# Second attention: the high and low parts of queries and keys are made by GpSimd from a whole copy that ScalarE writes

## The chip, the cores and the metric

The kernel runs on one core of a Trainium2 chip. The metric is the device time of one execution in microseconds (us), the median of the runs shown. One execution was profiled; every row below is from it. Engines: PE is TensorE's matmul, PEld its weight load, DVE is VectorE, ACT is ScalarE, POOL is GpSimd, SP is SyncE, which issues all DMAs spoken of here.

## The reference, cut to what matters

Sixteen sequences of 512 rows by 256 columns go through four layers, each with a residual: a first attention, a feed-forward layer with FP4 rounding, a second attention, and the feed-forward layer again. The change is in the second attention alone:

```python
Q = einsum('bsh,nhd->bnsd', x, Wq) + bq        # 8 heads of 32
K = einsum('bsh,nhd->bnsd', x, Wk) + bk
V = einsum('bsh,nhd->bnsd', x, Wv) + bv
qq, kq = Q @ Wc2q + bc2q, K @ Wc2q + bc2q      # 8 numbers for each row and head
fid = (qq . kq) / max(|qq| |kq|, 1e-8)
qw = fid * (1 + 0.1 * sin(pi * fid))
cw = (Q . K) / sqrt(32)
probs = softmax(0.5 * qw + 0.5 * cw)
attn = (probs @ V) @ Wo + bo
x1 = layernorm(x + attn, g1, beta1)
qm = (x1 @ W1 + b1) @ Wm + bm
qe = tanh(qm) * cos(qm * pi / 4)
out = layernorm(x1 + (qe @ Wqo + bqo) @ W2 + b2, g2, beta2)
```

## The kernel before

The four layers run one after the other. In the second attention (`attention_b`) each engine has its own program, a loop of bodies `s` = -1 to 16, one for each sequence and some at the ends. The order of all work is written out by hand: a body has 16 slots `n`, each with four places `j`. Places of slots 0 to 7 hold the eight groups (two halves of heads `c`, four row tiles) of sequence s: `score_head` on PE, `total_max` on DVE, `exps` on ACT; the turning of the probabilities (`turn_head`, `move_turned`) and their product with V (`weigh`) lag one and two slots behind. Slots 8 to 15 hold the cosine term of the next sequence s+1: `dots` on PE, `sines` on ACT, `cosine_term` on DVE, two heads at a time, which hand the score banks from one engine to the next. Between these stand the side jobs of the list `B_JOBS`, one matmul group each into one of three PSUM banks (S, T0, T1), moved out by DVE or ACT as the two `MOVES` tables say. Those that matter here, with their place in PE's body:

```python
    (0, 3, "B0", "S", 1),     # code projections of sequence s+1
    (1, 3, "N0", "S", 1),     # their squared norms
    (5, 0, "G0", "S", 1),     # turns the inverse norms rn8, spread by GpSimd
    (5, 2, "R0", "S", 0),     # turns the inverse sums of the first half of heads
    (8, 1, "Q0", "S", 1), (9, 3, "K0", "T0", 1),     # queries, keys of s+1, half 0
    (10, 3, "y0", "S", 0), (11, 1, "y1", "T0", 0),   # output projection of s
    (13, 3, "Q1", "S", 1), (14, 1, "K1", "T0", 1),   # queries, keys of s+1, half 1
```

Scores are made from numbers split into a high part, rounded to the matmul's fp32r type, and a low part, the rest. For each of Q0, K0, Q1 and K1, ACT (line 2070) writes the high part `part[:, i, 0, :]`, the PSUM bank plus the bias, and DVE (line 1963) writes the low part `part[:, i, 1, :]`, the bank plus the bias less the high part, and frees the bank. When K of a half is freed, SP's `place(s, c)` (lines 1749 to 1756) copies the parts with six DMAs into `stack`, the operand of `score_head`; half 0 is wanted at slot 0 of the next body, half 1 at slot 4.

GpSimd's body is a fixed queue: `inverse_norms` (line 1831, a power; waits until N0 is moved), `spread_norms` (line 1818, writes `rn8`, which G0 reads), `spread_sums(s, 0)` (line 1827, for R0), `add_row2`, `low_part` (line 1835, the low part of the code units), `spread_sums(s, 1)`, `rstd_of(s + 2, 0)` (line 1799), `add_row1` (line 1842, waits until y1 is moved), `rstd_of(s, 1)` (line 1792), `applied(x1)` (lines 1807 to 1813), `rstd_of(s - 1, 2)`, `applied(x2)`, `residual` (line 1852).

Of the kernel before, what the change touches and what calls it, by code (L numbers as in the profile page):

```python
# [7 lines left out]
ALU = mybir.AluOpType  # L8
# [3 lines left out]
P = 128  # L12
# [1603 lines left out]
def attention_b(nc, s_passed, ident, consts, w, u, kept, front, x_from, x_to, head):  # L1616
    ctx = ExitStack()
    with ctx:
# [27 lines left out]
        hi, lo, units = head.hi, head.lo, head.units  # L1646
        part = sb("part", [P, 2, 2, SEQ], FP32R)
        stack = sb("stack", [P, 2, 2, 4, SEQ], FP32R)
        v = sb("v", [P, TILES, H])
        negmax = sb("negmax", [P, B_GROUPS, 4])  # L1650
        sums = sb("sums", [P, 2, TILES, 4])
# [29 lines left out]
        s_xr = sem("residual_input_ready")  # L1681
        s_sq, s_rn, s_rn8 = head.s_sq, head.s_rn, head.s_rn8
        s_uhi, s_ulo, s_qs = head.s_uhi, head.s_ulo, head.s_qs
        s_hi = sem("high_part_ready")
        s_placed = sem("parts_placed")
        s_dots = sem("dots_ready")
        s_sin = sem("sines_ready")
# [33 lines left out]
        @block.sync  # L1721
        def _(sp):
            def one(ap, q):
                return ap.rearrange("s (t p) h -> p (s t) h", p=P)[:, bass.ds(q * TILES, TILES), :]

            def load_next(q):
                wait(sp, s_xh, 4 * q)
                sp.dma_start(xin[:], one(x_from, q)).then_inc(s_xin, 16)

            def load_again(q):  # L1730
                wait(sp, s_store, 16 * q)
                sp.dma_start(xres[:], one(x_from, q)).then_inc(s_xres, 16)

            def store_x(q):
                sp.wait_ge(s_add, q + 1)
                sp.dma_start(one(x_to, q), xres[:]).then_inc(s_store, 16)

            def place_units(q):

                sp.wait_ge(s_uhi, q + 1)  # L1740
                sp.sem_inc(s_passed, 1)
                wait(sp, s_dots, 32 * q)
                for src, blocks_ in ((hi, ((0, 0), (0, 1), (1, 0), (1, 2))), (lo, ((0, 2), (0, 3), (1, 1), (1, 3)))):
                    if src is lo:
                        sp.wait_ge(s_ulo, q + 1)
                    for i, b in blocks_:
                        sp.dma_start(units[NQ * b:NQ * (b + 1), i, :, :], src[64 * i:64 * i + 64, :]).then_inc(s_qs, 16)

            def place(s, c):

                freed(sp, s, f"K{c}")
                sp.sem_inc(s_passed, 1)
                wait(sp, s_score, 32 * s + 16 + 16 * c)
                for i, order in enumerate(((0, 0, 1), (0, 1, 0))):
                    for b, h in enumerate(order):
                        sp.dma_start(stack[32 * b:32 * b + 32, i, c, :, :].bitcast(FP32),
                                     part[:, i, h, :].bitcast(FP32)).then_inc(s_placed, 16)

            def body(s):
                if has(s + 2):  # L1760
                    load_next(s + 2)
                if has(s) and has(s + 1):
                    place_units(s + 1)
                if has(s - 2):
                    store_x(s - 2)
                if has(s - 1):
                    load_again(s - 1)
                if has(s + 1):
                    place(s, 0)
                    place(s, 1)  # L1770
                if s == SEQS - 1:
                    sp.wait_ge(s_turn, 32 * s + 16)
                    sp.sem_inc(s_passed, 1)
                    for dst, src in kept:
                        sp.dma_start(dst, src).then_inc(s_kept, 16)
                    sp.wait_ge(s_turn, 32 * s + 28)
                    sp.sem_inc(s_passed, 1)
                    sp.dma_start(front.x_of(0), one(x_to, 0)).then_inc(front.s_x, 16)

            b_bodies(sp, body, 2)  # L1780
            store_x(SEQS - 1)
            sp.wait_ge(s_kept, 16 * len(kept))
            sp.wait_ge(s_store, 16 * SEQS)

        @block.gpsimd
        def _(pool):
# [28 lines left out]
            def spread_norms(q):  # L1815
# [3 lines left out]
                                 rn[:].rearrange("p (b h) -> p b h", h=B_HEADS).unsqueeze(2)  # L1819
                                 .to_broadcast([P, 2 * TILES, NQ, B_HEADS])).then_inc(s_rn8, 1)  # L1820

            def spread_sums(s, c):

                wait(pool, s_o, 2 * s + c)
                pool.wait_ge(s_inv, 2 * s + c + 1)
                src = inv_sums[:].rearrange("p t h -> p (t h)").unsqueeze(2).to_broadcast([P, 4 * TILES, HD])
                pool.tensor_copy(rec[:].rearrange("p t (h d) -> p (t h) d", d=HD), src).then_inc(s_rec, 1)
# [26 lines left out]
            def body(s):  # L1854
                if has(s) and has(s + 1):
                    inverse_norms(s)
                    spread_norms(s + 1)
                if has(s):
                    spread_sums(s, 0)
                if has(s - 1):  # L1860
                    add_row2(s - 1)
                if has(s) and has(s + 1):
                    low_part(s + 1)
                if has(s):
                    spread_sums(s, 1)
                if has(s + 2):
                    rstd_of(s + 2, 0)
                if has(s + 1):
                    add_row1(s)
                if has(s):  # L1870
                    rstd_of(s, 1)
                if s == SEQS - 1:
                    front.pool_norm(pool, 0)
                if s == SEQS:
                    front.pool_scale(pool, 0)
                if has(s):
                    applied(x1, s, 1, G1, BETA1, s_x1)
                if has(s - 1):
                    rstd_of(s - 1, 2)
                    applied(x2, s - 1, 2, G2, BETA2, s_x2)  # L1880
                    residual(s - 1)
                if s == SEQS - 1:
                    front.pool_divide(pool, 0)
# [4 lines left out]
        def _(dve):  # L1888
# [53 lines left out]
            def move_side(s, job):  # L1942
# [6 lines left out]
                if job == "z1":  # L1949
                    dve.tensor_copy(zT[:, 1, :], side).then_inc(done, 1)  # L1950
                elif job == "B0":
                    wait(dve, s_ulo, q)
                    dve.tensor_scalar(out=base[:], in0=side, scalar1=w["bqk"][:], scalar2=None,
                                      op0=ALU.add).then_inc(done, 1)
                elif job == "N0":
                    dve.tensor_scalar(out=n2[:], in0=side[:, 0:64], scalar1=NORM2_MIN, scalar2=None,
                                      op0=ALU.max).then_inc(done, 1)
                elif job == "G0":
                    dve.tensor_tensor(out=base[:], in0=base[:], in1=side, op=ALU.mult).then_inc(done, 1)
                elif job[0] in "QK":  # L1960
                    i = "QK".index(job[0])
                    dve.wait_ge(s_hi, 4 * q + 2 * c + i + 1)
                    dve.scalar_tensor_tensor(out=part[:, i, 1, :], in0=side, scalar=w[("bq", "bk")[i]][:, c:c + 1],
                                             in1=part[:, i, 0, :], op0=ALU.add, op1=ALU.subtract).then_inc(done, 1)
                elif job[0] == "y":
                    dve.wait_ge(s_xr, q + 1)
                    wait(dve, s_row2, q)
                    dve.tensor_tensor(out=x1[:, d, :], in0=pair, in1=xr[:, d, :], op=ALU.add).then_inc(done, 1)
                elif job == "m0":
                    dve.tensor_tensor(out=qm[:], in0=side[:, 0:TILES * NQ].rearrange("p (t q) -> p t q", q=NQ),  # L1970
                                      in1=w["bm"][:].unsqueeze(1).to_broadcast([P, TILES, NQ]),
                                      op=ALU.add).then_inc(done, 1)
                elif job == "t0":
                    dve.tensor_copy(qeT, side[0:NQ, :]).then_inc(done, 1)
                else:
                    dve.wait_ge(s_row2, q + 1)
                    dve.tensor_tensor(out=x2[:, d, :], in0=pair, in1=x2[:, d, :], op=ALU.add).then_inc(done, 1)
# [26 lines left out]
            def reciprocals(s, c):  # L2004
# [1 line left out]
                wait(dve, s_rec, 2 * s + c)  # L2006
                dve.reciprocal(out=inv_sums[:], in_=sums[:, c, :, :]).then_inc(s_inv, 1)

            MOVES = {(1, 0): "B0", (2, 0): "N0", (3, 3): "z1", (5, 1): "G0", (6, 3): "m0", (8, 3): "Q0", (10, 1): "K0", (10, 3): "t0",
                     (11, 1): "y0", (11, 3): "y1", (12, 1): "f0", (12, 3): "f1", (14, 1): "Q1", (14, 3): "K1"}  # L2010

            def body(s):
                for n in range(B_SLOTS):
# [34 lines left out]
        def _(act):  # L2048
            def move_side(s, job):
# [16 lines left out]
                    act.activation(zT[:, 0, :], side, ACT.Copy).then_inc(done, 1)  # L2066
                elif job[0] in "QK":
                    i = "QK".index(job[0])
                    wait(act, s_placed, 96 * (2 * q + c))
                    act.activation(part[:, i, 0, :], side, ACT.Identity,  # L2070
                                   bias=w[("bq", "bk")[i]][:, c:c + 1]).then_inc(s_hi, 1)
                elif job[0] == "V":
                    act.activation(v[:, 2 * c:2 * c + 2, :], side.rearrange("p (a h) -> p a h", a=2),
                                   ACT.Copy).then_inc(done, 1)
# [348 lines left out]
```

## Time and profile before

| | us |
|---|---|
| median of 3 runs | 3481.36 |
| lowest and highest run | 3473.24, 3483.72 |
| the profiled execution | 3484.37 |
| its span | 3482.6 |
| PE busy | 3049.3 (88%) |
| DVE busy | 2696.7 (77%) |
| ACT busy | 2123.2 (61%) |
| POOL busy | 1576.3 (45%) |

The shares are averages over four layers with different limits. Queries and keys of the second attention are moved between 1670 and 2847 us of the span, so a change there is read from that stage, one body after the other, and from what each engine waits for in it.

### The profile page before, as it was taken

What the parts mean: (1) busy time and instruction counts of PE and PEld (TensorE: products, weight loads), DVE (VectorE), ACT (ScalarE), POOL (GpSimd) and SP (SyncE); (2) the same over time, 40 slices, a digit from 0 to 9 for tenths busy, and PEclk for the clock granted to TensorE, in tenths of its full rate; (3) what the DMA queues carried; (4) which work ended last, traced back from release to release, by engine and by line L of the source; (5) the groups of instructions that cost most, each with busy time, mean ns of one, the idle gap of its engine ahead of it and who ended that gap; (6) DMA issues with size and microseconds to landing.
All of it is one profiled execution on the core that took longest, in us unless ns stands there. A gap on an engine that the chain in (4) does not pass through costs nothing. (4 is left out here: it accounts for less than half of the span.)

```text
span 3482.6 us, 70085 instructions
## 1 busy us (share of the span) xinstructions
PE 3049.3 (88%) x23640; PEld 2358.0 (68%) x23640; DVE 2696.7 (77%) x6902; ACT 2123.2 (61%) x5264; POOL 1576.3 (45%) x1287
## 2 busy tenths in 40 slices
PE   5998999999985999997789989888988993899998
PEld 3666666666664888887456656666665662788888
DVE  4666666666666999995688888888888883899997
ACT  3777777777772344343677777777778782344443
POOL 4323223232203555554135666655556655455554
PEclk9999999999996999998899999999999996999999
DMA  5354353543423000000434444444454441111100
GB/s 91 53 77 66 56 77 57 74 68 53 72 36 120 13 19 13 19 19 17 63 55 74 67 75 73 61 74 67 67 74 69 72 84 51 37 37 37 32 24 25
DMA packets 133654, 193.45 MB, mean 56 GB/s; under 512 B 15110, under 2 KB 81030, under 8 KB 132614
## 3 DMA queue, kind: packets, MB, share of 16 engines
q1 hardware_dynamic: 133302, 188.96, 31.8%
q8 instruction: 196, 3.21, 0.4%
q14 instruction: 156, 1.28, 0.2%
HBM read 45.12 MB, written 28.84 MB: 21 GB/s over the span
## 5 line engine op out<-in xcount | busy, mean ns | idle before, releaser
L476 ACT ACTIVATE a_probs<-a_probs,a_negmax 128x176 f32<-128x176 f32 (+4 forms) x1024 | 502.7, 491 | 250.5 <-DVE a_negmax L402 246.5
L402 DVE CUSTOM_DVE_ANT_0 a_probs<-a_mask,a_score 128x176 f32<-128x176 f32 (+4 forms) x1024 | 404.3, 400 | 308.2 <-PE a_turned L560 149.8
L560 PE MATMUL a_turned<-ident,a_probs 128*128 128x128 f32 (+1 forms) x2176 | 403.3, 279 | 52.2 <-DVE a_pT L411 25.6
L1996 DVE CUSTOM_DVE_ANT_0 b_u<-b_u,b_score 128x512 f32<-128x512 f32 x512 | 341.0, 682 | 130.1 <-PE b_score L2235 126.7
L2109 ACT ACTIVATE b_u<-b_u,b_negmax 128x512 f32<-128x512 f32 x512 | 367.1, 718 | 106.8 <-DVE b_negmax L1996 105.6
L1493 PE MATMUL f_y_bank<-f_wdT,f_hqT 128*128 128x256 f32 x1536 | 362.8, 387 | 41.7 <-ACT f_hqT L1424 38.3
L1288 POOL TENSOR_TENSOR f_hq<-f_h_mark,f_nscale 128x704 f32<-128x704 f32 x128 | 177.6, 1387 | 407.4 <-DVE f_h_mark L1357 407.4
L1988 DVE SCALAR_TENSOR_TENSOR b_u<-b_u,b_score 128x1024 f32<-128x1024 f32 x256 | 310.4, 1217 | 65.9 <-ACT b_u L2102 60.9
L2102 ACT ACTIVATE b_u<-b_score 128x1024 f32<-128x1024 f32 x256 | 261.9, 1024 | 158.6 <-PE b_score L2225 157.0
L1493 PEld LDWEIGHTS f_y_bank<-f_wdT,f_hqT 128*128 128x128 f32 x1536 | 288.7, 192 | 91.4 <-issue 56.8
L336 POOL COPY a_rec<-a_inv_sums 128x512 f32<-128x512 f32 x32 | 19.5, 610 | 703.4 <-DVE a_inv_sums L416 703.4
L2244 PE MATMUL b_turned<-ident,b_u 128*128 128x128 f32 x2048 | 318.0, 280 | 14.2 <-DVE b_pT L2002 10.5
L560 PEld LDWEIGHTS a_turned<-ident,a_probs 128*128 128x128 f32 (+1 forms) x2176 | 236.6, 134 | 127.7 <-ACT a_probs L476 62.7
L1417 ACT ACTIVATE f_h_mag<-f_hu 128x704 f32<-128x704 f32 x128 | 100.8, 788 | 333.0 <-POOL f_hu L1280 333.0
L2244 PEld LDWEIGHTS b_turned<-ident,b_u 128*128 128x128 f32 x2048 | 245.7, 143 | 85.4 <-issue 47.9
L1476 PE MATMUL f_gate<-f_wguT,f_xqT 128*128 128x352 f32 x1536 | 286.0, 336 | 0.0
L1476 PE MATMUL f_up<-f_wguT,f_xqT 128*128 128x352 f32 x1536 | 280.7, 332 | 0.0
L2235 PE MATMUL b_score<-b_stack 96*128 96x512 f32 x512 | 256.9, 513 | 25.5 <-DVE b_u L1988 25.5
L1476 PEld LDWEIGHTS f_gate<-f_wguT,f_xqT 128*128 128x128 f32 x1536 | 251.8, 194 | 0.2
L1476 PEld LDWEIGHTS f_up<-f_wguT,f_xqT 128*128 128x128 f32 x1536 | 248.0, 191 | 0.0
L411 DVE COPY a_pT<-a_turned 128x256 f32<-128x256 f32 (+3 forms) x512 | 223.8, 437 | 3.6 <-PE a_turned L560 1.4
L551 PE MATMUL a_score<-a_stack_k,a_stack_q 112*128 112x512 f32 (+3 forms) x512 | 207.3, 416 | 1.5 <-DVE a_negmax L402 1.5
(271 smaller groups left out, 7274.0 us busy)
## 6 DMA issues: line engine op xcount, KB each, us to landing
b_stack<-b_part SPq DMA_DIRECT2D x192, 256.0 KB, 7.8
a_stack_q<-a_part SPq DMA_DIRECT2D x192, 128.0 KB, 4.4
a_wide_k<-a_part SPq DMA_DIRECT2D x96, 164.0 KB, 7.8
a_stack_k<-a_part SPq DMA_DIRECT2D x96, 128.0 KB, 4.7
xs<-in_x_dram SPq DMA_DIRECT2D x16, 512.0 KB, 10.4
x_before_b<-xs SPq DMA_DIRECT2D x16, 512.0 KB, 2.9
b_units<-b_hi_lo SPq DMA_DIRECT2D x128, 64.0 KB
b_xres<-x_before_b SPq DMA_DIRECT2D x16, 512.0 KB, 3.8
```

What stands on the lines that cost most here:

```text
L402: dve.tensor_tensor_reduce(out=probs[:, n % 2, j, 0:keys(n)], in0=mask_of(n), in1=score[j][:, 0:keys(n)], scale=-1.0, scalar=3.0e38, op0=A ...
L411: dve.tensor_copy(pT[:, n % 2, j, 0:t, :], turned[0][:, 0:t, :]).then_inc(s_mv_v, 1)
L476: act.activation(probs[:, n % 2, j, 0:keys(n)], probs[:, n % 2, j, 0:keys(n)], ACT.Exp, bias=negmax[:, n, j:j + 1], scale=-1.0, accum_out= ...
L560: m = nc.tensor.transpose(turned[j % 2][0:rows, u, :], chunk(n, probs[:, n % 2, j, :], u), ident[:])
L1476: m = mm(dst[:, a, 0:HALF], xqT[:, i, k, t * P:(t + 1) * P], wguT[:, j, k, at:at + HALF], start=p == 0, stop=p == len(products) - 1)
L1493: m = mm(y_bank[:, 0:H], hqT[:, t % 2, c * P:(c + 1) * P], wdT[:, c, :], start=c == 0, stop=c == IC - 1)
L1988: dve.scalar_tensor_tensor(out=u[:, g, d, :], in0=u[:, g, d, :], scalar=10.0, in1=score[:, d, :], op0=ALU.add, op1=ALU.mult).then_inc(s_u, 1)
L1996: dve.tensor_tensor_reduce(out=u[:, n, j, :], in0=u[:, n, j, :], in1=score[:, j, :], scale=-0.05, scalar=3.0e38, op0=ALU.add, op1=ALU.min, ...
L2102: act.activation(u[:, g, d, :], score[:, d, :], ACT.Sin, scale=PI_IN).then_inc(s_sin, 1)
L2109: act.activation(u[:, n, j, :], u[:, n, j, :], ACT.Exp, bias=negmax[:, n, j:j + 1], scale=-1.0, accum_out=sums[:, c, t, j:j + 1]).then_inc ...
L2235: mm(score[:, j, :], stack[0:96, 0, c, j, t * P:(t + 1) * P], stack[0:96, 1, c, j, :], start=True, stop=True).then_inc(s_score, 1)
L2244: m = nc.tensor.transpose(turned[j % 2][:, t, :], u[:, n, j, t * P:(t + 1) * P], ident[:])
```

## The change

ACT writes the whole value, bank plus bias, to a new fp32 buffer `whole_part[:, i, :]`, waits for its own write, frees the bank, and raises `s_whole`. GpSimd gets two calls of a new function `split`, one for each half `c`: for queries and then keys it copies the whole value to the high part, waits for that, and subtracts the high part from the whole value into the low part. The calls stand behind `spread_sums(s, 1)` and behind `applied(x1)`. The four moves of DVE are gone, also from its `MOVES` table. SP's `place` waits for the second low part of a half in place of the freed bank.

```diff
+        whole_part = sb("whole_part", [P, 2, SEQ])
...
             def place(s, c):
 
-                freed(sp, s, f"K{c}")
+                sp.wait_ge(s_low, 2 * (2 * (s + 1) + c + 1))
...
+            def split(q, c):
+
+                wait(pool, s_placed, 96 * (2 * q + c))
+                for i in range(2):
+                    step = 2 * (2 * q + c) + i + 1
+                    pool.wait_ge(s_whole, step)
+                    pool.tensor_copy(part[:, i, 0, :], whole_part[:, i, :]).then_inc(s_hi, 1)
+                    pool.wait_ge(s_hi, step)
+                    tt(out=part[:, i, 1, :], in0=whole_part[:, i, :], in1=part[:, i, 0, :],
+                       op=ALU.subtract).then_inc(s_low, 1)
...
                     spread_sums(s, 1)
+                if has(s + 1):
+                    split(s + 1, 0)
                 if has(s + 2):
                     rstd_of(s + 2, 0)
...
                     applied(x1, s, 1, G1, BETA1, s_x1)
+                if has(s + 1):
+                    split(s + 1, 1)
                 if has(s - 1):
                     rstd_of(s - 1, 2)
...
-                elif job[0] in "QK":
-                    i = "QK".index(job[0])
-                    dve.wait_ge(s_hi, 4 * q + 2 * c + i + 1)
-                    dve.scalar_tensor_tensor(out=part[:, i, 1, :], in0=side, scalar=w[("bq", "bk")[i]][:, c:c + 1],
-                                             in1=part[:, i, 0, :], op0=ALU.add, op1=ALU.subtract).then_inc(done, 1)
...
                     i = "QK".index(job[0])
-                    wait(act, s_placed, 96 * (2 * q + c))
-                    act.activation(part[:, i, 0, :], side, ACT.Identity,
-                                   bias=w[("bq", "bk")[i]][:, c:c + 1]).then_inc(s_hi, 1)
+                    wait(act, s_low, 2 * (2 * q + c - 1) + i + 1 if 2 * q + c else 0)
+                    act.activation(whole_part[:, i, :], side, ACT.Identity,
+                                   bias=w[("bq", "bk")[i]][:, c:c + 1]).then_inc(done, 1)
+                    freed(act, s, job)
+                    act.sem_inc(s_whole, 1)
```

## Rows read from the trace of the kernel before

**Rows 1.** Groups by line, 1900 to 2800 us: count, busy, mean; idle before, releaser.

```profile
L1963 DVE SCALAR_TENSOR_TENSOR b_part<-b_turned,b_bk,b_part 128x512 fp32r<-128x512 f32 x24 | 17.9, 746 | 0.0
...
L1827 POOL COPY b_rec<-b_inv_sums 128x512 f32<-128x512 f32 x23 | 14.1, 612 | 184.1 <-DVE b_inv_sums L2007 183.9
...
L1835 POOL TENSOR_TENSOR b_hi_lo<-b_base,b_hi_lo 128x512 f16<-128x512 f32 x11 | 12.8, 1164 | 16.3 <-ACT b_hi_lo L2060 16.3
```

**Rows 2.** POOL's groups by line and shape, whole span; columns as in rows 1.

```profile
L296 POOL TENSOR_TENSOR a_square<-a_square 128x512 f32<-128x512 f32 x15 | 19.1, 1272 | 1.2
...
L286 POOL MEMSET a_stack_q<- 128x8192 f32 x1 | 6.9, 6925 | 0.0
```

**Rows 3.** Timeline of POOL, one body: start, us, instruction [idle before and releaser].

```profile
2210.24 1.02 POOL L1799 TENSOR_TENSOR b_rstd<-b_vare,consts 128x4 f32<-128x4 f32 x1 [5.50 <-DVE b_vare L1904]
...
2219.67 2.36 POOL L1842 TENSOR_TENSOR b_xr<-b_xh_xT,b_rows 128x1024 f32<-128x1024 f32 x1 [8.14 <-DVE b_x L1968]
2222.56 0.23 POOL L1792 TENSOR_SCALAR b_vare<-b_mv 128x4 f32<-128x4 f32 x1 [0.53 <-DVE b_mv L1898]
...
2233.72 0.25 POOL L1792 TENSOR_SCALAR b_vare<-b_mv 128x4 f32<-128x4 f32 x1
...
2247.39 10.54 POOL L1831 TENSOR_TENSOR b_rn<-b_n,consts 128x64 f32<-128x64 f32 x1
2257.99 0.61 POOL L1818 COPY b_rn<-b_rn 128x512 f32<-128x512 f32 x1
```

**Rows 4.** Timeline of PE: the job G0 in five bodies.

```profile
1799.47 0.60 PE L2180 MATMUL b_spare<-ident,b_rn 128*128 128x128 f32 x4
...
2182.98 0.60 PE L2180 MATMUL b_spare<-ident,b_rn 128*128 128x128 f32 x4
...
2260.34 0.60 PE L2180 MATMUL b_spare<-ident,b_rn 128*128 128x128 f32 x4
...
2490.00 0.61 PE L2180 MATMUL b_spare<-ident,b_rn 128*128 128x128 f32 x4
...
2797.68 0.60 PE L2180 MATMUL b_spare<-ident,b_rn 128*128 128x128 f32 x4
```

**Rows 5.** Timeline of POOL ahead of the fourth G0 of rows 4.

```profile
2489.23 0.61 POOL L1818 COPY b_rn<-b_rn 128x512 f32<-128x512 f32 x1
```

**Rows 6.** Timeline of ACT around Q0, and behind K0.

```profile
2205.08 0.69 ACT L2070 ACTIVATE b_part<-b_spare,b_bq 128x512 fp32r<-128x512 f32 x1
2205.65 1.03 ACT L2102 ACTIVATE b_u<-b_score 128x1024 f32<-128x1024 f32 x1
...
2214.46 1.02 ACT L2102 ACTIVATE b_u<-b_score 128x1024 f32<-128x1024 f32 x1 [1.46 <-PE b_score L2225]
```

**Rows 7.** Timeline of DVE around Q0, and behind K0.

```profile
2205.88 0.75 DVE L1963 SCALAR_TENSOR_TENSOR b_part<-b_spare,b_bq,b_part 128x512 fp32r<-128x512 f32 x1
2206.72 1.22 DVE L1988 SCALAR_TENSOR_TENSOR b_u<-b_u,b_score 128x1024 f32<-128x1024 f32 x1
...
2215.52 1.22 DVE L1988 SCALAR_TENSOR_TENSOR b_u<-b_u,b_score 128x1024 f32<-128x1024 f32 x1
```

**Rows 8.** Busy us (instructions) by stretch: PE, PEld, DVE, ACT, POOL; granted clock, DMA, GB/s.

```profile
2222.56:2260.34 37.78, 32.83 (x239) 22.31 (x240) 31.48 (x72) 31.05 (x65) 36.93 (x21) 0.91 0.52 70
2232.36:2235.78 3.42, 1.75 (x6) 0.81 (x7) 3.25 (x4) 3.40 (x5) 3.23 (x4) 1.00 0.49 93
2235.78:2239.19 3.41, 3.41 (x7) 1.46 (x5) 2.18 (x8) 2.96 (x9) 3.41 (x4) 0.50 1.06 122
2299.93:2336.34 36.41, 32.23 (x244) 22.10 (x243) 31.47 (x72) 31.23 (x65) 35.57 (x20) 0.94 0.54 73
2310.87:2321.11 10.24, 7.41 (x38) 5.01 (x39) 8.88 (x21) 9.36 (x21) 9.89 (x9) 1.00 0.96 124
```

**Rows 9.** The tile `b_part`: how long its DMAs took.

```profile
DMA to landing us min/median/max: 4.2/7.8/12.0
```

**Rows 10.** Timeline of PE: the first score of half 1 in the next body.

```profile
2255.12 0.48 PE L2235 MATMUL b_score<-b_stack 96*128 96x512 f32 x1
```

More of the change, by code:

```diff
@@ L1683, in attention_b @@
         s_uhi, s_ulo, s_qs = head.s_uhi, head.s_ulo, head.s_qs
+        s_whole = sem("whole_part_ready")
         s_hi = sem("high_part_ready")
+        s_low = sem("low_part_ready")
         s_placed = sem("parts_placed")
@@ L2007, in reciprocals @@
                 dve.reciprocal(out=inv_sums[:], in_=sums[:, c, :, :]).then_inc(s_inv, 1)
-            MOVES = {(1, 0): "B0", (2, 0): "N0", (3, 3): "z1", (5, 1): "G0", (6, 3): "m0", (8, 3): "Q0", (10, 1): "K0", (10, 3): "t0",
-                     (11, 1): "y0", (11, 3): "y1", (12, 1): "f0", (12, 3): "f1", (14, 1): "Q1", (14, 3): "K1"}
+            MOVES = {(1, 0): "B0", (2, 0): "N0", (3, 3): "z1", (5, 1): "G0", (6, 3): "m0", (10, 3): "t0",
+                     (11, 1): "y0", (11, 3): "y1", (12, 1): "f0", (12, 3): "f1"}
             def body(s):
```

## The prediction

> **What bounds the kernel now.** I read the groups by line first: in the second attention DVE spends 0.746 us on each low part, 64 in all [rows 1], and DVE is the engine that these moves burden. That looks like 64 x 0.746 = 47.7 us to be had. The question is whether any of it lies on the path, so I read POOL's timeline over one body next, then PE's, and then the stretches between.
>
> POOL has gaps in the front of a body: 5.50 us ahead of `rstd_of(s + 2, 0)`, 8.14 us ahead of `add_row1` [rows 3], and 184 us of waiting in 900 us ahead of `spread_sums` [rows 1]. Then, from 2222.56 (`rstd_of(s, 1)`, released by DVE's statistics of x1) to the end of `spread_norms` at 2258.60, it runs without a gap that counts: busy 36.93 of the 37.78 us to PE's job G0 [rows 3, 8]. What it makes last there, `rn8`, is what G0 reads, and G0 starts at 2260.34 [rows 4]. So there is a loop: G0 on PE, then 39.58 us (2182.98 to 2222.56) to POOL's `rstd_of(s, 1)`, then 36.04 us of POOL's queue to `rn8`, then G0 again [rows 3, 4]. POOL's two legs are 75.62 us. A body takes (2797.68 - 1799.47) / 13 = 76.79 us, over the 13 intervals from the second G0 to the fifteenth [rows 4]. POOL thus has 1.2 us a body to spare on average; in the tightest body `rn8` was ready at 2489.84, 0.16 us ahead of G0 at 2490.00 [rows 4, 5]. By the share of busy time POOL seems idle more than half the time; by this loop it is as near to the bound as PE.
>
> **The change part by part.** *POOL, half 1.* `split(s + 1, 1)` comes between `applied(x1)`, which ends at 2233.72, and the second `rstd_of` [rows 3], in the middle of the gapless run. Its inputs don't hold it up: the timeline has ACT done with Q1 and K1 some 2 us before. It is two copies and two subtractions of 128x512, each step waiting for the one before. The trace has a POOL copy of that size at 0.612 us, with a spread source [rows 1], and a subtraction with one f16 operand at 1.164 us [rows 1]. Each hand-over costs about 0.08 us, as between POOL's own dependent steps (estimate from 2247.39 + 10.54 to 2257.99 [rows 3], 0.06, rounded up). I take 2 x (0.612 + 1.164 + 0.16) = 3.87 us. Neither row is this operation exactly. Bounds: below, a memset's rate for the copy, 6.925 / 16 = 0.433 us [rows 2], gives 3.51; above, 1.272 us [rows 2] for all four, gives 5.41. Both middle values are of the same size and engine, so I stay there.
>
> The GPSIMD Engine Reference of the Trainium skill (Performance versus the Vector engine) prices an elementwise pass by cycles: some 1.8 an element with one input and 2.6 with two, so an estimate from that page is 0.77 and 1.11 us for 512. By that page the split would be 4.1 us and the sum 3 us more; the page also says that VectorE is about twice as fast at this, and rows 1 show 1.56 times for a two-input pass (1.164 against 0.746).
>
> What is queued behind it all moves back: the statistics step and apply of x2, `residual`, the power of 10.54 us, `spread_norms` [rows 3]. `rn8` comes 3.87 us later; 1.2 of it is spare, the rest PE waits at G0. Behind `spread_norms` stand `spread_sums(s, 0)` for R0, two places after G0, then `add_row2` and `low_part`; they follow `rn8` as closely as now while PE starts later, so they add nothing. The store of the row block is later and nobody waits for it.
>
> *POOL, half 0.* `split(s + 1, 0)` falls in the gaps of 5.50 and 8.14 us [rows 3]. Q0 is done some 0.9 us, and K0 about 7 us, behind `spread_sums`; I put its end near 2213.8, and `rstd_of(s + 2, 0)`, now at 2210.24 to 2211.26, then ends near 2215. ACT normalises with it only in slot 13, behind y1, and `add_row1`, next in the queue, waits for y1 until 2219.67 anyway [rows 3]. Cost 0; without that cover 3.87 us.
>
> *DVE.* Four moves of 0.746 us go from each body. Behind Q0 the next cosine term starts at 2206.72, right as ACT's sine ends (2205.65 + 1.03 = 2206.68) [rows 6, 7]: it waits for ACT, not for the move. Behind K0 the same holds one step on: 2215.52 against 2214.46 + 1.02 = 2215.48, a sine that itself waited for PE [rows 6, 7]. So the leg of 39.58 us gets nothing back. Q1 and K1 lie behind 2222.56, in the leg where POOL decides and DVE has slack. Gain 0; its bound is 4 x 0.746 a body.
>
> *ACT.* The activation has the same size, but now ACT waits for its own write before it goes on. Between Q0 and the next sine there are now 0.57 us (2205.08 to 2205.65), though Q0 lasts 0.69 [rows 6]: with the wait the sine starts after 0.69 plus a hand-over, some 0.2 us later, and this sine is on the leg. The trace has no such wait of ACT; bounds 0.1 (the overlap alone) and 0.5. K0 is followed by an idle ACT; Q1 and K1 lie in POOL's leg. I take 0.2 a body. ACT's other wait, for the low part before last, is long met.
>
> *Banks and SP.* ACT frees the bank earlier than DVE did; PE is not held there in the leg that counts. `place` of half 0 starts at about the same time. `place` of half 1 waits until 2233.72 + 3.87 = 2237.6; six DMAs issue in some 4 us and land at worst 12.0 us later [rows 9], at 2253.6, ahead of the score at 2255.12 [rows 10]. Were they late, the first 2 us would vanish in the wait at G0 behind it. Behind `place` SP has the load of the sequence after next, wanted 40 us later. Cost 0.
>
> *The sum.* The loop becomes 39.58 + 0.2 + 36.04 + 3.87 + 0.16 = 79.85 us, 13 times 1038.0, against 998.2 now: +39.8 us. The interval before has no x2 in POOL's queue and stays.
>
> *The clock.* PE now idles at G0 for about 2.3 to 3.7 us in each body (40.1 us behind `rstd_of`, against arrivals at 36.41 and 37.78 [rows 8]). In 2232.36 to 2235.78 PE was busy 1.75 of 3.42 us, and behind it the granted clock was 0.50, 1.2 GHz [rows 8]. In 2310.87 to 2321.11 it idled 2.8 us in pieces and kept 1.00, 2.4 GHz [rows 8]. A leg with more time at the lower level (0.91) took 37.78 us, one with less (0.94) 36.41 [rows 8]: 1.37 us for one more such drop. Falls that now lie in POOL's leg are hidden; one behind G0 falls in the leg that PE bounds. I count 1.37 us in eight of ten bodies: 13 x 0.8 x 1.37 = +14 us. TensorE: Matmul & The Clock Gate of the Trainium skill (HAM oscillation) says that a wait paid in every round can bring the array back to the lower clock every time; by it the term is 18 us.
>
> The profiled execution took 3484.37 us, 3.0 above the median of 3481.36. In all +54 us: 3538 on its scale, 3535 on the median's.
>
> **The rivals.** *The loop without the clock:* the wait comes but PE keeps 1.00; +40, 3521 us. *A dear split:* the copy costs like the 1.272 us row; with the clock falling in every body 39.78 + 36.04 + 5.41 + 0.16 + 1.37 = 82.76, 13 x 82.76 - 998.2 = +78, 3559 us. *Faster:* DVE's moves are on the path of slots 8 to 15 and the split is hidden. For it speaks that DVE is busy there almost without a gap; against it, that the cosine terms start as the sines end [rows 6, 7] and that POOL's run has no gap. It would need a split of under 1.2 us a body, where the cheapest bound is 3.51; then at most 47.7 us come back, 3434 us. *No change:* PE's legs give back what G0 waits, because PE finds other idle time to catch up; 3481 to 3490. PE has waits in its leg of 39.58, but they are for DVE and ACT results that move with PE.
>
> **How the numbers follow.** Forecast, loop with clock: 0.58. Loop without the clock: 0.20. Dear split: 0.14. No change: 0.05. Faster: 0.03. The predicted time is 3535. The low end is the cheap split with neither wait of ACT nor clock: 13 x (39.58 + 36.04 + 3.51 + 0.16) - 998.2 = +32.6, 3514, less some scatter of the runs: 3509. The high end is the dear split: 3561. A measurement tells about 0.3%, 10 us, from no change; slower 0.92, same 0.05, faster 0.03.
>
> **What would show it.** Right: PE idle at G0 (line 2180) released by POOL, 2 to 4 us in each of 13 bodies; body to body 79.8 to 81.3 us; POOL without a gap from `rstd_of(s, 1)` to `spread_norms`, about 39.9 us; DVE's idle time larger by more than 48 us; a granted clock of 0.50 soon after G0. Wrong: if G0 finds `rn8` waiting, POOL's loop is not the bound and the DVE moves were; if copy or subtraction last longer than 0.61 and 1.16, the size is off; if the leg of 39.58 gets shorter by over 0.3, DVE was on its path; if half 1 is late, PE waits at line 2235 for DMAs of line 1756's successor.

## The result, and the profile after

The changed kernel takes 3559.27 us (median of 4 runs, 3552.83 to 3559.84) against 3480.58 us of the kernel before (median of 4): ratio 1.022, 95% interval 1.0205 to 1.0234, slower by 79 us. The forecast was 3535 us in a range of 3509 to 3561. The profiled execution took 3559.76 us.

The page of the kernel after, busy time by engine:

```profile
PE 3076.2 (86%) x23640; PEld 2376.3 (67%) x23640; DVE 2661.0 (75%) x6838; ACT 2128.6 (60%) x5264; POOL 1694.5 (48%) x1415
```

VectorE has 64 instructions fewer, GpSimd 128 more; 118.2 us more of GpSimd are 1.85 us for each of the 64 pairs of a high and a low part. The two groups of the split, by line, from 1600 to 3000 us (count, busy, mean; idle before):

```profile
L1833 POOL TENSOR_TENSOR b_part<-b_whole_part,b_part 128x512 fp32r<-128x512 f32 x64 | 81.6, 1275 | 5.2
...
L1831 POOL CAST b_part<-b_whole_part 128x512 fp32r<-128x512 f32 x64 | 39.1, 610 | 107.4 <-ACTq L2086 107.3
```

The copy cost what the spread copy did, the subtraction what the dearer of the two rows did [rows 1, 2]. GpSimd's timeline over one body of the kernel after:

```profile
2257.38 0.23 POOL L1795 TENSOR_SCALAR b_vare<-b_mv 128x4 f32<-128x4 f32 x1 [0.53 <-DVE b_mv L1916]
...
2268.53 0.62 POOL L1831 CAST b_part<-b_whole_part 128x512 fp32r<-128x512 f32 x1
2269.24 1.28 POOL L1833 TENSOR_TENSOR b_part<-b_whole_part,b_part 128x512 fp32r<-128x512 f32 x1
...
2272.40 0.24 POOL L1795 TENSOR_SCALAR b_vare<-b_mv 128x4 f32<-128x4 f32 x1
...
2286.04 10.54 POOL L1845 TENSOR_TENSOR b_rn<-b_n,consts 128x64 f32<-128x64 f32 x1
2296.65 0.61 POOL L1821 COPY b_rn<-b_rn 128x512 f32<-128x512 f32 x1
```

Read it against [rows 3]: from the first statistics step to the second one 15.02 us where there were 11.16, the split's 3.86; then the same steps; `rn8` is ready 39.88 us behind the first where it was 36.04. On PE's timeline, four of its G0 jobs:

```profile
1802.28 0.60 PE L2195 MATMUL b_spare<-ident,b_rn 128*128 128x128 f32 x4
...
1883.79 1.08 PE L2195 MATMUL b_spare<-ident,b_rn 128*128 128x128 f32 x4 [1.36 <-POOL b_rn L1821]
...
2297.41 1.08 PE L2195 MATMUL b_spare<-ident,b_rn 128*128 128x128 f32 x4 [2.59 <-POOL b_rn L1821]
...
2873.15 0.63 PE L2195 MATMUL b_spare<-ident,b_rn 128*128 128x128 f32 x4 [1.65 <-POOL b_rn L1821]
```

G0 now waits for GpSimd: in the body shown it starts at 2297.41, 0.15 us behind `rn8` at 2297.26, where before `rn8` lay ready [rows 4]. It waits 0.97 to 3.44 us in 12 of the 14 bodies from the second to the fifteenth, and not at all in two. The same in sum, in the list of waits from 1900 to 2900 us (total, times, longest):

```profile
PE b_spare L2195 <- POOL b_rn L1821: 24.1, 11, 3.4
```

The 13 intervals from the second G0 to the fifteenth take 1070.87 us (1802.28 to 2873.15) against 998.21: +72.7 of the 75.4 us by which the spans differ (3558.0 against 3482.6). A body is 82.37 us, of which GpSimd's leg is 39.85 on average, as forecast (39.91). The excess is in the other leg, from G0 to the statistics step: 42.27 us on average, from 39.90 to 44.19, against 39.58 before. What makes it long is seen in stretches (busy us of PE, PEld, DVE, ACT, POOL; granted clock, DMA, GB/s):

```profile
1802.28:1832.58 30.30, 26.71 (x290) 19.22 (x289) 23.27 (x57) 24.06 (x49) 6.77 (x8) 1.00 0.22 36
1832.58:1835.99 3.41, 3.41 (x10) 2.32 (x9) 1.82 (x3) 0.71 (x1) 1.20 (x3) 0.50 0.66 114
...
1881.10:1883.70 2.60, 1.05 (x7) 0.52 (x5) 2.37 (x6) 2.60 (x7) 2.54 (x3) 1.00 0.00 0
1883.80:1887.18 3.38, 3.38 (x33) 2.78 (x37) 1.29 (x3) 1.01 (x3) 2.72 (x2) 0.50 0.00 0
...
2129.57:2136.40 6.83, 6.10 (x49) 4.96 (x50) 2.24 (x6) 2.04 (x5) 4.63 (x4) 0.50 0.04 9
...
2793.28:2833.18 39.90, 35.72 (x325) 24.87 (x325) 30.58 (x71) 27.68 (x51) 11.86 (x12) 1.00 0.39 70
```

The last is a whole leg in which the clock keeps 2.4 GHz (1.00): 39.90 us. In the body of 1883.79 PE stands at G0, the clock is at 1.2 GHz (0.50) right behind it, and the leg takes 41.60 us. That was expected. In the body of 1802.28, where G0 did not wait, the clock falls 30 us later, and the leg takes 41.55 us. That was not. Of the 13 legs nine have a fall that begins around G0 (from 1.8 us ahead of it to 0.5 us behind), six one some 30 us behind it, two neither. In five of the nine the lower level lasts 6.83 us, as around the G0 of 2130.30, a leg of 42.99 us; three of them have another fall some 40 us behind G0, ahead of the end of the leg. A leg with one fall alone that lasts 3.41 us takes 41.48 to 41.60 us, so such a fall costs 1.6 to 1.7 us. By that price six falls of the second kind are some 10 of the 31 us by which the 13 legs exceed 39.90 (estimate); nearly all the rest goes to the falls around G0 and the late ones, 2.3 us for each of the nine legs.

What PE did ahead of the second kind of fall, and ACT before that (timelines of ACT in one body and of PE in another, at the same place):

```profile
2322.39 0.69 ACT L2083 ACTIVATE b_whole_part<-b_spare,b_bq 128x512 f32<-128x512 f32 x1
2323.26 1.02 ACT L2117 ACTIVATE b_u<-b_score 128x1024 f32<-128x1024 f32 x1 [0.17 <-ACT b_whole_part L2083]
```

```profile
1830.91 0.60 PE L2240 MATMUL b_score<-b_units 96*128 96x512 f16 x2 [1.58 <-DVE b_u L2001]
```

Behind Q0 the next sine starts 0.87 us after the activation's start, where it was 0.57 [rows 6]: ACT waits for its own write. PE then waits 1.58 us at one place in slot 10; in the body of [rows 3] the same wait was 0.97 us, with another of 0.27 us ahead of it, for VectorE's move of Q0, which is gone (timeline of PE in the kernel before):

```profile
2206.69 0.66 PE L2190 MATMUL b_spare<-ident,b_rec 128*128 128x128 f32 x4 [0.27 <-DVE b_part L1963]
...
2211.34 0.60 PE L2225 MATMUL b_score<-b_units 96*128 96x512 f16 x2 [0.97 <-DVE b_u L1988]
```

VectorE is not held up by GpSimd's longer work: in this stage no step of VectorE of the changed kernel lasts over 0.04 us more than the shortest of its line and shape, although GpSimd works 118 us longer than before.

### The profile page after: what moved, and what is told of

It reads as the page before. It is cut to its first block and busy times, and to the rows that moved or that the text cites. A ratio compares the mean times of both kernels' runs of the same rounds, so it can differ in the third digit from the quotient of the medians.

```text
span 3558.0 us, 70180 instructions
## 1 busy us (share of the span) xinstructions
PE 3076.2 (86%) x23640; PEld 2376.3 (67%) x23640; DVE 2661.0 (75%) x6838; ACT 2128.6 (60%) x5264; POOL 1694.5 (48%) x1415
## 5 line engine op out<-in xcount | busy, mean ns | idle before, releaser
L2259 PE MATMUL b_turned<-ident,b_u 128*128 128x128 f32 x2048 | 325.7, 284 | 13.8 <-DVE b_pT L2015 10.0
L2250 PE MATMUL b_score<-b_stack 96*128 96x512 f32 x512 | 269.3, 538 | 27.3 <-DVE b_u L2001 25.1
```

Of the source, the lines that this page charges most:

```text
L2250: mm(score[:, j, :], stack[0:96, 0, c, j, t * P:(t + 1) * P], stack[0:96, 1, c, j, :], start=True, stop=True).then_inc(s_score, 1)
L2259: m = nc.tensor.transpose(turned[j % 2][:, t, :], u[:, n, j, t * P:(t + 1) * P], ident[:])
```

## The experiments

All against the kernel before, run beside them on the same chip. The chips differ from one group of runs to the next (medians of the kernel before: 3482.24, 3481.40 and 3477.62 us), so differences are compared and not times. The queue theory is that of the forecast. The changed kernel is +78.7 us.

**GpSimd's time alone.** The kernel before, its moves kept, and the split's four instructions on spare data that nobody reads:

```diff
+            def idle_split(q):
+                for i in range(2):
+                    step = 4 * q + 2 * i + 1
+                    wait(pool, s_dummy, step)
+                    pool.tensor_copy(spare_part[:], spare_in[:]).then_inc(s_dummy, 1)
+                    pool.wait_ge(s_dummy, step + 1)
+                    tt(out=spare_part[:], in0=spare_in[:], in1=spare_part[:],
+                       op=ALU.subtract).then_inc(s_dummy, 1)
...
                     applied(x1, s, 1, G1, BETA1, s_x1)
+                if has(s + 1):
+                    idle_split(s + 1)
```

> The kernel before with all its moves, and GpSimd does two copies and two subtractions of 128x512 on spare data at the place where the second split stands (behind the apply of x1); nobody waits for them, and the output is unchanged. The queue theory (what costs is GpSimd's time ahead of the spread norms that G0 reads): 36.04 to 39.9 us from the statistics of x1 to the spread norms, G0 waits, the clock falls behind it, 3535 to 3555 us. The rival (ScalarE's wait for its own write, or the later hand-over of the parts, costs the time): no such wait here, so 3471 to 3491 us.

Measured 3539.63 us, ratio 1.0171 (1.0156 to 1.0186), +57 us. In its list of waits, 1900 to 2900 us:

```profile
PE b_spare L2197 <- POOL b_rn L1821: 43.4, 12, 3.9
```

Nearly three quarters of the loss come from GpSimd work that produces nothing and touches no one's data. The rival is out as the main cause; some 21 us are left for it.

**Half 0 alone, half 1 alone.** The other half is moved as before, by ACT and DVE; each has only its call of `split`:

```diff
                     spread_sums(s, 1)
-                if has(s + 1):
-                    split(s + 1, 0)        # left out in the second of the two
...
-                if has(s + 1):
-                    split(s + 1, 1)        # left out in the first of the two
```

> Only half 0 (Q0, K0) goes the new way; Q1 and K1 are moved by VectorE as before. The queue theory: this split lies in GpSimd's gaps, so GpSimd's leg stays at 36.0 us and only some 0.3 us a body is added behind Q0 by ScalarE's wait: 3478 to 3492 us. The ScalarE theory: this half has the wait of ScalarE that lies on the path (Q0), so most of the 79 us comes: 3520 to 3560 us.

> Only half 1 (Q1, K1) goes the new way; Q0 and K0 are moved by VectorE as before. The queue theory: GpSimd's leg is 39.9 us and G0 waits, so nearly all of the loss is here: 3535 to 3558 us. Where in this range tells how much of the clock's second fall, 30 us behind G0, hangs on Q0's wait of ScalarE: 3535 if all of it, 3555 if none. The ScalarE theory: its waits behind Q1 and K1 are off the path, 3478 to 3492 us.

Half 0: 3498.57 us, 1.0048 (1.0033 to 1.0063), +16 us. Half 1: 3532.84 us, 1.0146 (1.0129 to 1.0163), +51 us. Both say which half costs what: half 1, with its split in the gapless run, most; half 0, with its split in the gaps, little. Together they are 67 of the 79 us. Half 1 lies 2 us under its range. Half 0 is dearer than the 0.3 us a body that I gave it, and lies 7 us over its range; the split itself is not the reason, as GpSimd's leg is 36.0 to 36.7 us there and was 36.0 to 36.6. One leg of the half 0 kernel, and the fall inside another (columns as above):

```profile
1793.19:1833.06 39.87, 35.71 (x327) 24.85 (x325) 31.61 (x73) 28.69 (x54) 10.32 (x11) 1.00 0.36 56
...
1900.70:1904.05 3.35, 3.35 (x9) 2.28 (x8) 2.29 (x3) 0.47 (x1) 1.68 (x3) 0.50 0.49 94
```

A leg with the clock up is 39.87 us: the wait itself costs 0.29. With a fall 29 to 30 us behind G0 it is 41.55, in 9 of its 13 legs. With half 1 alone no leg has a fall there.

**Without ACT's wait for its own write.** GpSimd waits for the freed bank instead, which the same write raises:

```diff
                                    bias=w[("bq", "bk")[i]][:, c:c + 1]).then_inc(done, 1)
-                    freed(act, s, job)
-                    act.sem_inc(s_whole, 1)
...
-                    pool.wait_ge(s_whole, step)
+                    freed(pool, q - 1, f"{'QK'[i]}{c}")
```

> The changed kernel, but ScalarE doesn't wait for its own write: GpSimd waits for the freed bank itself, which the same write raises. The queue theory: GpSimd's leg stays at 39.9 us; the other leg loses 0.3 us a body and some falls of the clock: 3540 to 3556 us. The ScalarE theory: the loss goes with the wait, 3480 to 3505 us.

Measured 3541.54 us, 1.0173 (1.0158 to 1.0188), +59 us: the wait is worth 19 us of the 79. With the 57 us of GpSimd's spare work that makes 77 of them. GpSimd's leg stays, 39.89 us on average. The timeline of PE in this run at the place of slot 10:

```profile
2070.50 0.61 PE L2237 MATMUL b_score<-b_units 96*128 96x512 f16 x2 [1.31 <-DVE b_u L2000]
```

1.31 us in place of 1.58 (1.43 in one body), and none of its 13 legs has a fall 30 us behind G0. So here this fall comes only with ACT's wait of 0.3 us, and where it comes it adds 1.7 us to the leg (41.55 against 39.87 in the run with half 0).

**PE kept busy while it waits.** Sixteen turns of the identity into G0's free bank, read by nobody, just ahead of the wait:

```diff
                 elif job[0] == "G":
+                    for k in range(16):
+                        nc.tensor.transpose(side[:, (k % TILES) * P:(k % TILES + 1) * P], ident[:], ident[:])
                     pe.wait_ge(s_rn8, q + 1)
```

> The changed kernel, and PE turns the identity 16 times (some 2 us of work that nobody reads) into G0's free bank just ahead of its wait for the spread norms. The clock theory: PE's stand at G0 is what lets the granted clock fall behind it, so with the same GpSimd leg of 39.9 us the fall behind G0 goes in most bodies, at 1.6 us each in 9 bodies: 3538 to 3552 us, faster though PE does more. The rival (the time behind G0 is lost to something else, or the fall comes anyway): 3556 to 3570 us.

> The changed kernel without ScalarE's wait, and with the 16 turns of the identity on PE ahead of G0. Both falls of the clock in the leg from G0 should be gone, and what is left is the queue alone, 13 times 3 us: 3516 to 3530 us. If the clock's falls are not what the two edits took away, 3538 us and more.

In the changed kernel: 3542.12 us, 1.0184 (1.0164 to 1.0205), +61. That is 18 us less of a loss by the medians and some 13 by the ratios, though PE does more. None of its 13 legs has a fall around G0 any more; seven still have the one 30 us behind it. The stretches behind one G0 that waited 0.83 us (columns as above):

```profile
2200.26:2229.80 29.54, 25.74 (x283) 18.36 (x283) 21.05 (x54) 21.61 (x43) 7.55 (x8) 1.00 0.23 55
2229.80:2233.21 3.41, 3.32 (x9) 2.67 (x9) 2.93 (x3) 1.02 (x1) 2.03 (x3) 0.50 0.39 81
```

With ACT's wait gone too: 3525.14 us, 1.0131 (1.0118 to 1.0144), +47.5, and no leg has a fall of either kind. Together the two edits take 31 us off the loss; singly they took 19 and 18. The timeline of PE in the kernel with both, and the stretches of one body, G0 to the statistics step and on to the next G0:

```profile
2353.22 1.91 PE L2191 MATMUL b_spare<-ident 128*128 128x128 f32 x16
2354.98 0.66 PE L2194 MATMUL b_spare<-ident,b_rn 128*128 128x128 f32 x4
```

```profile
2275.42:2315.06 39.64, 35.75 (x325) 24.91 (x325) 30.50 (x70) 27.14 (x49) 11.93 (x11) 1.00 0.40 70
2315.06:2354.98 39.92, 34.38 (x255) 24.08 (x255) 31.43 (x72) 32.57 (x69) 38.92 (x24) 0.91 0.47 64
```

This is the loop of the forecast bare: 39.64 + 39.92 = 79.56 us a body, in nearly all of its bodies. 13 x (79.56 - 76.79) = 36 us. The 13 bodies of its profile take 41.7 us more than before, one of them 4.5 us longer than this loop. The profiled run, 3519.98, was the fastest of four; the other 6 us to the median's 47.5 I can't place.

**GpSimd's second norm one body later: a failure.** The rstd, apply of x2 and residual, 13.7 us from 2233.72 to 2247.39 in the body of [rows 3], go behind `low_part` of the next body, where GpSimd stood idle for 16.65 us, and `low_part` goes ahead of `add_row2`; in the changed kernel, in the kernel before, and in the changed kernel without ACT's wait:

```diff
+                if has(s) and has(s + 1):
+                    low_part(s + 1)
+                if has(s - 2) and s < SEQS:
+                    second_norm(s - 2)
                 if has(s - 1):
                     add_row2(s - 1)
-                if has(s) and has(s + 1):
-                    low_part(s + 1)
...
-                if has(s - 1):
-                    rstd_of(s - 1, 2)
-                    applied(x2, s - 1, 2, G2, BETA2, s_x2)
-                    residual(s - 1)
+                if s >= SEQS - 1:
+                    second_norm(s - 1)
```

> The changed kernel, but GpSimd does the second norm's steps (rstd, apply of x2, residual, 13.4 us) of a sequence one body later, behind the low part of the code units, where it stood idle for 16 us. The queue theory: the spread norms no longer wait for them, G0 doesn't wait, and what is left is ScalarE's wait and the clock's fall 30 us behind G0, as with half 0 alone: 3485 to 3505 us. The rival (the split costs by its length wherever it stands, by the shared memory ports or GpSimd's sum of work): 3540 to 3560 us.

> The kernel before with the same later second norm, and no split. GpSimd's leg gets over 2 us of slack. The queue theory: the spread norms were ready 0.2 to 2.1 us ahead of G0 already, so nothing or little: 3465 to 3486 us.

> The changed kernel with the later second norm and without ScalarE's wait for its own write: both costs found so far are gone, and VectorE is without its four moves. If these moves were off the path, as predicted, it is like the kernel before with the later norm, within 10 us: 3465 to 3490 us. The rival (VectorE's moves were on the path, and their gain was covered by the two costs): 47.7 us at most come back, 3430 to 3462 us.

Measured 3592.47 (1.0323, 1.0305 to 1.0342), 3554.64 (1.0216, 1.0199 to 1.0232) and 3562.99 us (1.0242, 1.0224 to 1.0261): all far above what I expected, the kernel before by 73 us, with no split in it. Timelines of DVE, of POOL and of PE in that one, at the same time:

```profile
2214.37 0.19 DVE L1975 TENSOR_TENSOR b_qm<-b_spare,b_bm 128x32 f32<-128x32 f32 x1
...
2216.28 2.05 DVE L1931 TENSOR_SCALAR b_turns<-b_qm 128x32 f32<-128x32 f32 x1
2218.37 0.18 DVE L1934 TENSOR_SCALAR b_whole<-b_turns 128x32 f32<-128x32 f32 x1
2218.59 2.21 DVE L1937 TENSOR_TENSOR b_turns<-b_turns,b_whole 128x32 f32<-128x32 f32 x1
```

```profile
2215.91 2.39 POOL L1813 TENSOR_TENSOR b_x<-b_x,b_rows 128x1024 f32<-128x1024 f32 x1
2218.37 2.37 POOL L1852 TENSOR_TENSOR b_xres<-b_x,b_xres 128x1024 f32<-128x1024 f32 x1
```

```profile
2222.44 1.86 PE L2249 MATMUL b_turned<-ident,b_u 128*128 128x128 f32 x8 [4.03 <-DVE b_pT L2007]
```

Two steps of 32 elements that take 0.18 us elsewhere take 2.05 and 2.21 us and end with GpSimd's pass (2218.33 against 2218.30, 2220.80 against 2220.74). They stand in slot 7 ahead of score work that PE waits for, here 4.03 us. In all, 24 such steps in 12 bodies last 46.9 us longer than elsewhere, so they can account for 47 of the 73 us; the rest I did not resolve. The changed kernel without ACT's wait is 8 us above the kernel before with the same later norm, within the 10 that I allowed; but with steps of DVE stretched like this these runs can't say much on whether its moves were on the path.

**Only the last two steps later.** The add of beta2 and the residual, 4.7 us, end ahead of slot 7: without ACT's wait; in the kernel before; with ACT's wait.

```diff
+                if has(s) and has(s + 1):
+                    low_part(s + 1)
+                if has(s - 2) and s < SEQS:
+                    second_tail(s - 2)      # add of BETA2, residual
                 if has(s - 1):
                     add_row2(s - 1)
-                if has(s) and has(s + 1):
-                    low_part(s + 1)
...
-                    applied(x2, s - 1, 2, G2, BETA2, s_x2)
-                    residual(s - 1)
+                    applied(x2, s - 1, 2, G2, None, s_x2)
+                    if s >= SEQS - 1:
+                        second_tail(s - 1)
```

> The changed kernel without ScalarE's wait for its own write, and only the last two steps of the second norm (add of beta2, residual, 4.7 us) stand one body later, behind the low part of the code units; they end some 4 us before VectorE's small steps of the middle part, which the 13.4 us of the earlier try ran into. The queue theory: GpSimd's leg is 36.04 - 4.75 + 3.87 = 35.2 us and then waits for N0, G0 doesn't wait; VectorE's moves were off the path, so it is like the kernel before: 3470 to 3490 us. The rival (VectorE's moves were on the path): 3432 to 3464 us. The ports theory (GpSimd beside VectorE in slots 5 to 7 costs by itself): 3500 us and more.

> The kernel before with the same two steps later, and nothing else. GpSimd then always waits for N0; the spread norms come 0.4 us sooner in the bodies where they were last, 0.16 us ahead of G0 already. Queue theory: no change beyond the noise, 3468 to 3486 us. The ports theory: 3500 us and more.

> The changed kernel with the same two steps later, ScalarE's wait kept. What is left is that wait and the clock's fall 30 us behind G0, as with half 0 alone (+16 us): 3486 to 3506 us by the queue theory; 3530 to 3560 us if the wait at G0 stays.

Measured 3486.79 us (1.0021, 1.0012 to 1.0031), 3478.03 (0.9998, 0.9989 to 1.0006) and 3507.39 (1.008, 1.0067 to 1.0092). In the first GpSimd waits for N0, and DVE's small step is short again (timelines of POOL and DVE):

```profile
2243.46 10.54 POOL L1849 TENSOR_TENSOR b_rn<-b_n,consts 128x64 f32<-128x64 f32 x1 [0.64 <-DVE b_n L1985]
```

```profile
2270.51 0.18 DVE L1955 TENSOR_SCALAR b_turns<-b_qm 128x32 f32<-128x32 f32 x1
```

A leg from G0 to the statistics step in that first run, to be held against the 39.58 us from 2182.98 to 2222.56 in the kernel before (columns as above):

```profile
2179.45:2219.04 39.59, 35.70 (x327) 24.86 (x325) 31.61 (x73) 28.59 (x54) 16.20 (x13) 1.00 0.38 69
```

With both costs gone the changed kernel is 9 us above the kernel before, 0.12 to 0.31%, a remainder that I did not trace. The leg takes what it took, 39.6 us in nine of 13 bodies, although the moves of Q0 and K0 have left VectorE; and of the 47.7 us that VectorE's four moves a body would have given back on the path, nothing shows. They were off it. The kernel before gains nothing from the edit. With ACT's wait kept 30 us remain, 3507.39 us just over the expected 3506: seven of 13 legs have the fall 30 us behind G0, and its profile, of the slowest of six runs, has two bodies with a stall of PE of over 2 us inside `weigh` for which the trace names no releaser. No version tried beats the kernel before.

## Why the prediction was right, and where its size was short

*GpSimd's loop:* right. Leg 39.85 us for 39.91, hand-over to G0 0.14 for 0.16. That the split took 3.86 us for 3.87 is luck: two errors cancel. The subtraction was 1.275 us and not 1.164, 0.22 us too little for two; the four hand-overs took 0.09 us in all, 3.86 - 2 x (0.610 + 1.275), and not 0.32. The prediction's other pair of prices, 0.77 and 1.11 us, missed both ways: the copy took 0.610 us, the subtraction 1.275.

*ACT's wait:* 0.3 us a body in a leg with the clock up, for 0.2; the sine behind Q0 is on the path, as forecast.

*Loop without clock:* 13 x (39.85 + 0.14 + 39.90) - 998.2 = +40.4 us, forecast +39.8.

*The clock:* the term that was too small. 13 x (42.27 - 39.90) = 31 us, forecast 14. The fall behind G0 came about as often as said (nine of 13) but costs 1.6 to 1.7 us alone, and 2.3 on average with the legs in which the lower level lasted 6.83 us or came back late, where I took 1.37. What the forecast lacked is the second fall, 30 us behind G0, some 10 us: I costed ACT's wait at its 0.2 us and did not ask what PE's waits at slot 10 would then add up to. The early release of the bank, which I costed at nothing, may have helped it along: it took away the wait of 0.27 us ahead, and PE came to the next wait sooner. That this part counts beside ACT's wait is argued, not shown: no run has the early release with DVE's moves kept, or ACT's wait without the early release. That ACT's wait is needed is shown, nearly: without it the fall is gone from all 13 legs in two runs and comes in one of 13 in a third, behind a wait of 1.43 us at slot 10.

*The rest:* 75.4 - 40.4 - 30.8 leaves 4 us: 2.8 ahead of the second G0, and one body with 1.4 us more between `rn8` and G0.

*VectorE's moves off the path, half 0 hidden, SP's hand-over hidden:* right. Half 0 alone has GpSimd's leg at 36.0 to 36.7 us, against 36.0 to 36.6 before. The parts of half 1 held PE once, by 1.6 us, in the whole stage.

*The rivals:* the loop without the clock, which did not come here, is what the kernel with both edits shows in its bodies; the dear split was off in its price, 3.86 us against 5.41, and right in its time (3559), by luck, as the clock made up the difference; faster and no change are out.

*The range and the signs:* the measured 3559 us lie inside the range only because its high end, 3561, was set for the dear split, which did not come. Of the signs, a body of 79.8 to 81.3 us missed, as it was 82.4 on average (79.9 to 84.6), and so did a wait in each of 13 bodies; GpSimd's gapless 39.9 us, the longer idle time of DVE and the clock of 0.50 behind G0 came.

## What to carry to other kernels

An engine that is idle for half of its time can still close the loop: follow one body from the first result that the engine waits for to the result that the next body wants from it, and count what stands in its queue between, before moving work there. The place in the queue decided here: four instructions on spare data in the gapless run cost 57 us, while the split in the gaps left GpSimd's leg as it was, and the 16 us of that half go with ACT's wait and the clock. A wait of a few tenths on the path is to be priced with what PE's clock does behind it; and one edit that only fills the wait can show how much of a loss is the clock's.

## What the runs showed of the hardware that was not expected

Two of VectorE's small steps whose operands all lie in SBUF stood still while GpSimd ran a pass: 2.05 and 2.21 us for 0.18 and 0.19, until the pass ended. A step of the same size that reads PSUM (line 1975) took 0.19 us beside such a pass. SBUF — State Buffer of the Trainium skill (Who interferes with whom) says that the two engines share a port pair as an exclusive lock, held for a whole instruction, and that a VectorE step with two SBUF inputs, or in a two-port mode, contends for it with a GpSimd step that reads SBUF. The body shown agrees: the two steps end within 0.06 us of the pass.

A wait of PE of 1.31 us at slot 10 was followed by no fall of the clock in the run without ACT's wait, 12 legs, nor did one of 1.43 us in the thirteenth bring one; waits of 1.58 to 1.86 us at the same place were followed by a fall in six of 13 legs of the changed kernel and nine of 13 with half 0 alone. The fall did come once behind 1.43 us, in the run with the last two steps later. And 16 useless turns ahead of a wait, 1.91 us of PE's time, took 13 to 18 us off the changed kernel.
